# Gate and up projections of an FFN as Strassen block products on one NeuronCore

## What is computed

```
x = x + attention(layernorm(x))          # causal, one head of 64, 1024 x 1024 scores
y = layernorm(x)                          # 8 x 1024 tokens, 512 features
up_gate = y @ W1.T                        # W1: 2048 x 512
up_lin  = y @ W3.T                        # W3: 2048 x 512
hidden  = fwht(silu(up_gate) * up_lin)    # normalised Hadamard transform over 2048
out = x + hidden @ W2.T                   # W2: 512 x 2048
```

## Time and profile before

| | us |
|---|---|
| median of 3 runs | 2430.12 |
| profiled execution, its own time | 2429.33 |
| profiled execution, span in the trace | 2427.5 |
| mean granted TensorE clock | 0.995 |

### The profile page before, as it was taken

How to read it: one execution, slowest core, us unless ns; L and a number is a source line. 1 busy time by engine, 2 the same in 40 slices (tenths; PEclk the granted TensorE clock), 3 DMA queues, 4 the chain that set the end, 5 groups by cost and what they waited for, 6 DMA issues and landing times.

```text
span 2427.5 us, 30334 instructions
## 1 busy us (share of the span) xinstructions
PE 2311.7 (95%) x11890; PEld 1123.2 (46%) x11890; DVE 1259.7 (52%) x2887; ACT 935.6 (39%) x1469; POOL 175.4 (7%) x115
## 2 busy tenths in 40 slices
PE   2588899999999999999999999999999999999999
PEld 1244444444444544445444444445444454444444
DVE  7865554554555455454545545554554545555412
ACT  2646523334243433435333442434334353434411
POOL 4422200000000000000000000000000000000000
PEclk9989999999999999999999999999999999999999
DMA  6121110100101010000101001010100001010000
GB/s 254 44 79 47 41 53 1 53 1 5 48 1 53 1 53 1 19 34 1 53 1 53 1 9 45 1 53 1 53 1 30 24 1 53 1 44 1 10 9 18
DMA packets 35854, 75.58 MB, mean 31 GB/s; under 512 B 3968, under 2 KB 3968, under 8 KB 35200
## 3 DMA queue, kind: packets, MB, share of 16 engines
q1 hardware_dynamic: 35712, 73.65, 8.8%
HBM read 56.85 MB, written 16.78 MB: 30 GB/s over the span
## 4 chain that ended last, share of the span: by engine, by line
PE 83%; DVE 7%; ACT 2%; issue 1%; DVEq 0%; ACTq 0%
PE PU L551 8%; PE PD L592 8%; PE PU L552 8%; PE PU L553 8%; PE PD L594 8%; PE PD L593 8%; PE PG L551 8%; PE PG L552 8%; PE PG L553 8%; DVE ring L1328 2%; PE XY L382 1%; PE XY L396 1%; PE XY L411 1%; PE XY L431 1%; PE XY L381 1%
## 5 line engine op out<-in xcount | busy, mean ns | idle before, releaser
L1314 DVE SCALAR_TENSOR_TENSOR hd<-PU,afs,sil 128x512 f32<-128x512 f32 x256 | 191.8, 749 | 461.7 <-PE PU L553 443.6
L551 PE MATMUL PG<-xnT,WA 128*128 128x512 f16 x1024 | 390.0, 381 | 0.0
L551 PE MATMUL PU<-xnT,WA 128*128 128x512 f16 x1024 | 389.8, 381 | 0.0
L552 PE MATMUL PG<-xnT,WA 128*128 128x512 f16 x1024 | 389.4, 380 | 0.0
L553 PE MATMUL PG<-xnT,WA 128*128 128x512 f16 x1024 | 389.2, 380 | 0.0
L552 PE MATMUL PU<-xnT,WA 128*128 128x512 f16 x1024 | 388.8, 380 | 0.0
L592 PE MATMUL PD<-W2s,hT 128*128 128x512 f16 x1024 | 388.7, 380 | 0.0
L553 PE MATMUL PU<-xnT,WA 128*128 128x512 f16 x1024 | 388.6, 379 | 0.0
L593 PE MATMUL PD<-W2s,hT 128*128 128x512 f16 x1024 | 388.1, 379 | 0.0
L594 PE MATMUL PD<-W2s,hT 128*128 128x512 f16 x1024 | 388.1, 379 | 0.0
L858 ACT ACTIVATE sil<-PG,afs 128x512 f32<-128x512 f32 x256 | 175.5, 686 | 413.6 <-PE PG L553 412.5
(11 more groups left out here) (248 smaller groups left out, 2565.8 us busy)
## 6 DMA issues: line engine op xcount, KB each, us to landing
ring<-x SPq DMA_DIRECT2D x64, 256.0 KB, 3.5
out<-ring SPq DMA_DIRECT2D x64, 256.0 KB, 2.1
xraw<-xT SPq DMA_DIRECT2D x62, 256.0 KB, 3.5
W2s<-w SPq DMA_DIRECT2D x16, 512.0 KB, 13.7
raw<-w SPq DMA_DIRECT2D x32, 256.0 KB, 2.6
WA<-w SPq DMA_DIRECT2D x4, 1024.0 KB, 13.4
xnT<-small SPq DMA_DIRECT2D x1, 961.0 KB, 4.8
cosT<-tab SPq DMA_DIRECT2D x1, 512.0 KB, 12.5
```

The costliest lines, as they stand in the source:

```text
L551: pe.matmul(bank, wh, xa, start=k == 0, stop=False)
L552: pe.matmul(bank, wh, xb, start=False, stop=False)
L1314: ve.scalar_tensor_tensor(hd[:, :], U, afs[:, 16 + h:17 + h], sil[:, :], ALU.mult, ALU.mult).then_inc(v_hd, 1)
```

## The change

The main loop runs over eight sequences of 1024 tokens (NS) and 16 blocks, 128 steps `k`. In a step the gate and up rows of one block, the two halves of the 512 features and the two halves of the tokens are a 2 x 2 by 2 x 2 block product. It is made by Strassen's seven products: seven sums of weight blocks (`WF`, its split in `WS`), seven of token blocks (`XF`), 6 matmuls for each product, and sums of products in PSUM. Products 0, 2, 4 and 6 add up in bank 0 of PF; between them ScalarE copies the bank (`copy_b`), VectorE adds it to product 1 (`sum_c`, `sum_e`), and products 3 and 5 go on top of such copies. The four banks then hold up and gate of both token halves.

SBUF no longer holds all weights. The forms of the weights are made during the first sequence from W1 and W3 as loaded (already transposed by the host), written to DRAM by each step and loaded again for every step of the later sequences; split W2 likewise, a quarter at a time. The down product of four blocks runs in the four steps after them, into two PSUM banks, and each result is added to `ring` four times for each tile instead of once. The attention of chunk 1 runs ahead of the loop; the later chunks' 94 slots per sequence lie after the seven products of a step, at the places SLOTS. `outp` no longer normalises; `xnorm` does one slot later. `xtrans` transposes the f32 tile in four matmuls, and the split is made of the token forms. Weight transposes are gone; scales come as a matrix product (`scale_rows`).

```diff
+SLOTS = {z + (3 if z < 6 else 12): z for z in range(94) if z not in (9, 10)}
+BANK = (0, 3, 0, 1, 0, 2, 0)
...
             def xtrans(a, t):
-                w.wait_ge(v_x16, tile_no(a, t))
+                w.wait_ge(v_xs, tile_no(a, t))
                 w.wait_ge(*xfree)
-                for h in range(2):
-                    for j in range(4):
-                        i = pe.transpose(X16[:, (h * 4 + j) * 128:(h * 4 + j + 1) * 128], xnp[:, h, j * 128:(j + 1) * 128], id16[:, :])
+                for j in range(4):
+                    i = pe.transpose(X[:, j * 128:(j + 1) * 128], xs[:, j * 128:(j + 1) * 128], idn)
...
+            def product(k, i):
+                s, h = divmod(k, NH)
+                bank = PF[:, BANK[i], :]
...
+                    if k:
+                        w.wait_ge(v_hA, k)
+                if i == 1 and k:
+                    w.wait_ge(v_hE, k)
+                if i == 2:
+                    w.wait_ge(a_cb, k + 1)
+                if i == 4:
+                    w.wait_ge(v_c, k + 1)
+                if i == 6:
+                    w.wait_ge(v_e, k + 1)
+                for j in range(2):
+                    wh, wl = (WS[:, k % 2, m, WFORM[i], j * 128:(j + 1) * 128] for m in range(2))
+                    th, tl = (XF[:, m, i, j * 512:(j + 1) * 512] for m in range(2))
+                    pe.matmul(bank, wh, th, start=i < 2 and j == 0, stop=False, skip_group_check=True)
+                    pe.matmul(bank, wh, tl, start=False, stop=False, skip_group_check=True)
+                    m = pe.matmul(bank, wl, th, start=False, stop=j == 1, skip_group_check=True)
...
+            for slot in range(47):
+                attention(1, slot)
+                if slot in (9, 20):
+                    scale_rows(slot // 20)
+
+            for k in range(NK):
+                s, h = divmod(k, NH)
+                for i in range(7):
+                    product(k, i)
+                    if i in (1, 3, 5, 6):
+                        down(k, (1, 3, 5, 6).index(i))
+                    f = 7 * h + i
+                    if s + 1 < NS and f in SLOTS:
+                        attention(2 * s + 2 + SLOTS[f] // 47, SLOTS[f] % 47)
```

ScalarE in step k:

```diff
+                if k:
+                    high(k - 1)
+                copy_b(k)
...
+                fill(0)
+                copy_p5(k)
...
+                fill(1)
...
+                fill(2)
...
+                silu(k, 0)
+                fill(3)
...
+                fill(4)
+                silu(k, 1)
...
+                fill(5)
+                fill(6)
```

VectorE in step k (the first and the last step of a sequence also split and add token blocks):

```diff
+                if k:
+                    hidden(k - 1, 0)
+                    out_rows((k - 1) // 4 - 1, 2 * ((k - 1) % 4) + 1)
+                    low_part(k - 1)
...
+                fill(0)
...
+                fill(1)
...
+                sum_c(k)
...
+                fill(2)
+                fill(3)
+                out_rows(k // 4 - 1, 2 * (k % 4))
+                sum_e(k)
...
+                fill(4)
+                hidden(k, 1)
...
+                fill(5)
+                fill(6)
...
+            def hidden(k, i):
+                if i:
+                    w.wait_ge(a_sc2, k + 1)
+                    w.wait_ge(v_e, k + 1)
                 else:
+                    w.wait_ge(a_sb, k + 1)
+                    w.wait_ge(p_gu, gu_no(k, 6))
+                h = k % NH
+                ve.scalar_tensor_tensor(SH[:, i, :], PF[:, 3 * i, :], afs[:, 16 + h:17 + h], SH[:, i, :], ALU.mult,
+                                        ALU.mult).then_inc((v_hA, v_hE)[i], 1)
```

More of the change, by code:

```diff
@@ L49, in groups, with gu_no, xf_no, d_no @@
     return 1 + a % 2
[L52 to L62, removed]
+def gu_no(k, i):
+    return 7 * k + i + 1
+def xf_no(s, i):
+    return 7 * s + ((0, 2, 3, 1, 4, 5, 6)[i] if s == 0 else i) + 1
+def d_no(q, t):
+    return 8 * q + t + 1
 class Waits:
@@ L316, in _ @@
+            for t in range(8):
+                store(NS - 1, t)
+            for r in range(16):
+                w.wait_ge(d_out[r], 16 * (NS // 2))
         @block.tensor
@@ L573, in up @@
[L573 to L595 removed]
+                pe.matmul(Y[:, 0:256], ones.broadcast_to([128, 128]), dg[:, :], start=True, stop=True).then_inc(p_wb, 1)
@@ new lines, in _ @@
+            for slot in range(47):
+                attention(1, slot)
+                if slot in SPLIT:
+                    split2(SPLIT[slot])
+                if slot in (9, 20):
+                    scale_rows(slot // 20)
+                if slot in (17, 30):
+                    forms_high(slot // 30, 0)
+                    forms_high(slot // 30, 1)
+                if slot in (25, 26):
+                    tokens_high(0, (0, 3)[slot - 25])
+            for i in (1, 2, 4, 5, 6):
+                tokens_high(0, i)
@@ L967, in _ @@
+            high(NK - 1)
         @block.vector
@@ L1479, in _ @@
-            finish(NC - 1)
+            for j in (2, 10, 4, 12, 6, 14):
+                stats2_done = stat2(j)
+            for slot in range(47):
+                attention(1, slot)
+                if slot == 3:
+                    kept["scale2"] = scale2(stats2_done)
+                if slot in (18, 31):
+                    forms_low(slot // 31)
+                if slot in (25, 26):
+                    tokens_low(0, (0, 3)[slot - 25])
+            tokens_sum(0, 1)
+            tokens_low(0, 1)
@@ L1482, in _ @@
+            hidden(NK - 1, 0)
+            out_rows(NK // 4 - 2, 7)
+            low_part(NK - 1)
+            for t in range(8):
+                out_rows(NK // 4 - 1, t)
         @block.gpsimd
@@ new lines, in _ @@
+            for k in range(NK):
+                s, h = divmod(k, NH)
+                for j in range(7):
+                    f = 7 * h + j
+                    if s + 1 < NS and f in SLOTS:
+                        attention(2 * s + 2 + SLOTS[f] // 47, SLOTS[f] % 47)
+                    if s == 0:
+                        if j == 0 and 1 <= h < NH - 1:
+                            forms_low(h + 1)
+                        if j == 1 and 1 <= h < NH - 2:
+                            diagonals(h + 2)
+                        if j == 4 and h < NH - 2:
+                            forms(h + 2)
```

862 lines of the change are left out of this document (455 added, 407 removed).

## The result

| | before | after |
|---|---|---|
| median, 4 runs each, same chip | 2430.3 | 2851.79 (2848.16 to 2859.51) |
| ratio, 95% interval | | 1.174 (1.171 to 1.176) |
| profiled execution, its own time | 2429.33 | 2850.53 |
| its span | 2427.5 | 2848.7 |
| mean granted TensorE clock | 0.995 | 0.906 |

The change costs 421 us. The forecast was 2804, so 48 too low, inside its range.

What follows compares the result with a forecast made beforehand. TensorE, busy for 95% of the span, was taken to bound the kernel before. Start 225, TensorE's floor 2095, waits 417, clock 59, end 6 and 1.8 gave 2804 us; 2630 to 2870 had 60%, 2560 to 2940 8 in 10.

Steps and rivals of the forecast that it cites:

- the covers: Loop steps: TensorE waits where attention slots in VectorE's queue outlast its remaining work; 57 us per sequence, 417 in all.
- HA: VectorE's last product with the silu in a step; the next step's first product on TensorE waits for it.
- The clock: Half clock behind TensorE's long waits: four per sequence at 2.1 us each, 59 us in all.
- fp32 transposes: Token transposes in the loop's attention: four in fp32 take 0.94 us against 0.45 for eight f16, +27 us.
- The start: Chunk 1's attention runs alone before the loop; the FFN starts effectively at 225 us, bounds 210 and 240.
- The first sequence: From the first HA through 16 steps: 334 us, with 74 us of waits as weight forms are made.
- the loads of weights: Weights from DRAM, 0.9 MB a step: costed at nothing, hidden by 15 us of matmuls.
- VectorE's share of a sequence: Sign of being right: VectorE near 70% of a sequence, its total about 192 us in 266.
- scales: Row of scales as a matrix product on TensorE: 14 in the loop at about 0.5 us each, 7 us.
- the covers hold: Rival: VectorE reaches HA in time, so the kernel gets faster, centre 2370 us; chance 12%.
- half the waits: Rival: TensorE's loop waits come to 210 us, total 2563, from 2480 to 2630; chance 18%.
- a clock that stays low: Rival: waits of 3.5 us and more each cost 4 us of half speed, total 2870 to 2960; chance 10%.

Runs made afterwards that it cites:

- Experiment 1: Changed kernel with the attention slot at the last place of a step issued on VectorE after HA instead of before it: 2594.94 us.
- experiment 3: Changed kernel with one Newton round instead of three in the reciprocal root of the tile's statistics: 2739.3 us.
- experiment 4: Changed kernel with eight unused matmuls added ahead of the first product in the 14 steps that have a slot at the last place: 2763.75 us.
- experiments 5 and 7: Changed kernel, 5: GpSimd's low part of W2 left out, 2847.28 us; 7: five unused matmuls after each attention slot of chunk 1 before the loop, 2847.96 us.
- experiment 6: Changed kernel with most of GpSimd's weight forms for blocks 2 to 15 left out: 2830.12 us.
- experiment 2: Changed kernel with the attention slots at the last two places of a step both issued on VectorE after HA: 2599.84 us.

## Why the prediction was right

**The deciding term: the covers.** Right in mechanism and in size. I predicted a wait for HA in most steps; 14 of 16 have one. By place, predicted against measured in the sequence from 962.3: first normalisation, even, 6.7 and 6.47, odd, 4.35 and 3.25; even tiles 3.5 and 3.44 to 3.48; after the last even tile 3.2 and 3.01; odd tiles 2.1, 4.1, 4.5, 4.9 and 1.71, 3.12, 3.38, 5.25, each with the waits for `sum_e` that belong to it; rotations 4.6 and 3.64, 3.1 and 2.6; last projection 2.4 and 2.26. The 2.7 for the token splits did not come. In all 57 and 47.8: the queue walked, instruction by instruction, was a fifth too high. Experiment 1 shows that the cause is what stands ahead of HA in an in-order queue, and experiment 3 that the time of the piece goes over into the wait one to one.

**The clock.** Right in kind, less than half in size: 8.4 us predicted per sequence, 20.3 measured, of which 19.2 are matmuls at half clock; experiment 4 took away 13.7. The step that failed is the choice to charge only the four waits of 4.35 us and more: the clock fell 11 times in this sequence, twice of these for double the time, and the row at 1126 shows one such fall behind a wait of 2.26. The price of a fall was read too high: 0.61 over 4 us is 1.6 us lost and not 2.1, and a stretch of 3.4 us at half clock costs 1.7. I had written that with the even tiles "it would be twice that"; it is a little more.

**fp32 transposes.** This term was mis-sized: 27 us predicted, 0 measured.

```profile
1091.31 0.60 PE L507 MATMUL XY<-cst_s,xs 128*128 128x128 f32 x4
1091.75 0.39 PE L473 MATMUL XY<-id,Ph 128*128 128x128 f16 x4
```

Four take 0.44 us, the same as eight in f16, and they are recorded as four instructions, not eight. That they come out at the f16 price I had named as a sign of being wrong. The nearest row by type (an fp32 matmul of 64 columns) misled me; my lower bound was nearer. The phrase of the Trainium skill that I had set against it ("TensorE: Matmul & The Clock Gate", Terms, "4× faster for FP32") pointed the right way: 0.11 us each for 128 columns is a quarter of the 0.47 that two fp32 matmuls of 64 columns take by the earlier trace rows; against an f16 transpose (0.056) it is twice, and four take 0.44 and not the 0.22 that I had worked out from the phrase.

**The start.** Mis-sized by 27 us until the loop's middle, and by 5 more in the rest of that step. P4 of step 0 begins at 256.9, which with four products of 1.3 ahead of it makes 252 instead of 225:

```profile
256.89 0.38 PE L645 MATMUL PF<-XF,WS 128*128 128x512 f16 x1
```

That lies beyond my upper bound of 240, which I had named as a sign of being wrong. Four causes stand in the trace. The first normalisation takes 11.2 us (135.58 to 146.73) instead of 5.0, as the small VectorE instructions are stretched (next section). The scales' product waits for GpSimd, which has W2's splits queued ahead of it, and the first tile's output product stands behind that on TensorE:

```profile
175.73 1.22 PE L614 MATMUL XY<-dg,cst_s 128*128 128x256 f32 x2 [6.65 <-POOL dg L1665]
177.52 0.77 PE L498 MATMUL XY<-Mh,oh 128*128 128x512 f32 x1 [0.56 <-ACT sc L913]
```

TensorE's granted clock is 0.50 from 120 to 240. And at the loop's start it does not do four of seven products ahead of the token splits, as I had assumed, but two: the third waits for the copy of the bank, which ScalarE makes in order, behind the splits:

```profile
251.94 0.58 PE L645 MATMUL PF<-XF,WS 128*128 128x512 f16 x1 [7.07 <-ACT PF L943]
```

I had sized the token work but not asked what was queued behind it on the other engine. Its 16 us do not follow from what I wrote (nine times 1.3 is 11.7); that the trace has 15.9, from the last normalisation at 236.7 to the last low part's end at 252.6, is luck, for VectorE waits there for ScalarE's high parts. By experiments 5 and 7 GpSimd's low parts are worth 8 us of it and filling TensorE's pauses 3 to 5. The copy behind the splits was not tried by itself.

**The first sequence.** 362.6 instead of 334; experiment 6 shows that 25 us of it hang on GpSimd's weight forms. My 74 us of waits are not far off: 79.6 are named. The larger part of the 29 that are missing is the clock again: half clock loses 26.4 us against the 8.4 in the sum. I had counted what has to go through GpSimd, not what it does to VectorE meanwhile; how much of the 25 us is that stretching and how much is late products of scales, the run doesn't separate.

**Costed at nothing, and rightly:** the loads of weights. 0.9 MB land in 4.6 us in the median, and no wait of TensorE names one:

```profile
WS<-wscr SPq DMA_DIRECT2D x112, 896.0 KB, 4.6
```

The evictions of the down parts take 0.746 (L1457) and the sums between banks 0.70 (L1424) for 0.75, the steps of the last sequence 14.25, and the end 5.8 (26.5 less 96 matmuls) for 5.8, also as predicted. VectorE's share of a sequence is 57% and not the 70% that I named as a sign: its 187 us are close to my 192, but I had divided by a sequence without waits.

**The sum** came out 47 us low: start +32, first sequence +29, six sequences -14. That the six sequences come out right to 14 us is in part luck, for in them the errors cancel: waits -9 each, transposes -4, scales -1, clock +12. **The rivals:** that the covers hold fell with the first line of the waits; half the waits is what experiment 1 gives, but only in another order (2594.94, where the rival's sum was 2563); a clock that stays low did not come, 0.93 in a sequence.

## What to carry to other kernels

Removing matmuls from a TensorE-bound kernel also shortens the cover of each PSUM bank. Where the longest piece of in-order work ahead of the instruction that frees the bank is longer than that cover, the difference comes back as a wait (here 14.6 us per sequence were to be won, and 68 went to waits and the clock). Judge that by the piece (here 4.2 to 5 us against a cover of 1.3), not by the engine's total, and put the instruction that frees a bank first in its queue; moving one instruction of 0.75 us gave back 257 of 421 us. Count the clock behind a wait beside the wait itself (here 20 us on top of 48), and look at what every other engine's work does to the small instructions of the one that is critical.

## What the runs showed of the hardware

**GpSimd stretches small VectorE instructions, but only with some of its own.** The first normalisation in the start; GpSimd first, then VectorE beside it, and last one of the same VectorE line where GpSimd is idle:

```profile
135.96 2.47 POOL L1658 TENSOR_TENSOR ring<-ring,bb 128x512 f32<-128x512 f32 x2 [6.84 <-DVE st L1141]
138.43 1.57 POOL L1690 TENSOR_SCALAR H<-H,afs 128x512 f32<-128x512 f32 x1
140.09 1.15 POOL L1692 TENSOR_TENSOR W2S<-H,W2S 128x512 f16<-128x512 f32 x1
141.20 2.48 POOL L1658 TENSOR_TENSOR ring<-ring,bb 128x512 f32<-128x512 f32 x2
143.65 1.57 POOL L1690 TENSOR_SCALAR H<-H,afs 128x512 f32<-128x512 f32 x1
```

```profile
137.28 1.19 DVE L1105 TENSOR_SCALAR st<-st 128x4 f32<-128x4 f32 x1
...
139.36 0.16 DVE L1116 TENSOR_TENSOR st<-st 128x4 f32<-128x4 f32 x1
...
140.14 1.11 DVE L1118 SCALAR_TENSOR_TENSOR st<-st 128x4 f32<-128x4 f32 x1
141.29 1.18 DVE L1114 TENSOR_TENSOR st<-st 128x4 f32<-128x4 f32 x1
142.51 1.19 DVE L1116 TENSOR_TENSOR st<-st 128x4 f32<-128x4 f32 x1
143.73 0.63 DVE L1118 SCALAR_TENSOR_TENSOR st<-st 128x4 f32<-128x4 f32 x1
```

```profile
996.26 0.16 DVE L1116 TENSOR_TENSOR st<-st 128x4 f32<-128x4 f32 x1
```

An instruction on four columns takes 0.16 us alone and 1.1 to 1.2, the length of one GpSimd operation, while GpSimd works on two tensors. In the whole trace of the changed kernel, all 187 such instructions with GpSimd idle took 0.16 to 0.17 us, and of the 52 that lay beside nothing but GpSimd operations on two tensors 50 took over 0.4, with a median of 1.18. Beside GpSimd's product of one tensor with a column (138.43) they mostly keep their 0.16: six of the seven that began beside such a product did, and one took 0.63 (143.73). The Trainium skill ("SBUF — State Buffer", Who interferes with whom) says that a VectorE instruction with two SBUF inputs contends with a GpSimd instruction that reads SBUF, and that the shared port pair is an exclusive lock. The blocking for a whole instruction agrees with these rows. That it happens with any GpSimd instruction that reads SBUF mostly doesn't: beside the one with a single tensor input, six of seven were not stretched here. It also befell VectorE instructions with one tensor input (`TENSOR_SCALAR` at 137.28, 1.19 us), which by that section of the Trainium skill needs one of the faster modes; these rows can't tell whether it was in one.

**A pause of 2.3 us is mostly followed by half clock, but the length of the pause alone doesn't decide it.** From 640 to 2500 us of the changed kernel the clock fell behind every wait of 2.84 us or more and behind 9 of 11 waits of 2.26; behind the other two it stayed up for another 32 us. In experiment 1 it fell behind five of the six waits of 1.89 us, as behind the one that ends at 979.63 (the row below), and behind none of the six of 2.01 or 2.02 that came some 18 us before them:

```profile
980.00:984.00 4.00, 4.00 (x14) 0.61 0.00 0
```

In experiment 2 it fell behind only two of six waits of 3.26 or 3.27. What else decides it stays open. Behind the pause of 0.60 in experiment 1 the matmuls went on at full clock. Per sequence, waits of 48 us cost up to 20 more; keeping TensorE busy in part of them, with results that nobody uses, brought 88 us in a kernel of 2850.
